# A graph attention and mixture-of-experts kernel: probabilities divided before their transposes instead of after the attention product

## The reference

```
n = layernorm(x)
q, k, v = n @ Wq.T, n @ Wk.T, n @ Wv.T + bv          # 12 heads of 32
a = softmax(q @ k.T * 384**-0.5 + adj)                # per head; a row that is all zero gives zeros
x = x + (a @ v) @ Wo.T + bo
```

```
u = layernorm(x)
y = u + sum over the 2 chosen experts e of gate_e * (act_e(u @ w1[e] + b1[e]) @ w2[e] + b2[e])
x = x + layernorm(y) * ln_g + ln_b
```

## Time and profile before

| what | value |
| --- | --- |
| median of three runs | 1617.83 us |
| profiled execution, its own time | 1619.34 us |
| its span, first to last instruction | 1617.5 us |
| mean granted TensorE clock | 0.998 of full speed |
| TensorE busy (matmul) | 1586.6 us, 98% |
| VectorE, ScalarE, GpSimd busy | 1194.9, 970.5, 687.1 us |
| chain that ended last: TensorE | 89% of the span |
| attention loop | to about 705 us; VectorE, ScalarE and GpSimd are each 70 to 90% busy in it |
| experts | from 705 us on; GpSimd is 10% busy |

### The profile page before, as it was taken

One profiled execution on the slowest core, in us unless ns is written; L12 is line 12 of the kernel. 1 busy time (PEld: TensorE's weight loads), 2 busy tenths in 40 slices (PEclk: granted clock), 3 DMA queues, 4 the chain that ended last, 5 costly groups with the idle time before them and its releaser, 6 DMA issues.

```text
span 1617.5 us, 44743 instructions
## 1 busy us (share of the span) xinstructions
PE 1586.6 (98%) x12720; PEld 1524.0 (94%) x12720; DVE 1194.9 (74%) x3754; ACT 970.5 (60%) x2880; POOL 687.1 (42%) x1105
## 2 busy tenths in 40 slices
PE   8999999999999999989999999999999999999998
PEld 7999999999999999879999999999999999999998
DVE  5787788878887778777766666676777767677776
ACT  6899999988999988863433333344344433344442
POOL 3777887778777877731111111111111111111112
PEclk9999999999999999999999999999999999999999
DMA  5433333344444433682211111111111111111211
GB/s 181 161 121 124 104 118 116 130 155 152 155 158 145 152 132 116 211 341 84 60 59 53 56 59 60 56 59 61 61 60 46 60 60 56 60 60 52 67 47 45
DMA packets 93512, 163.87 MB, mean 101 GB/s; under 512 B 10305, under 2 KB 73793, under 8 KB 92097
## 3 DMA queue, kind: packets, MB, share of 16 engines
q1 hardware_dynamic: 91664, 145.01, 27.2%
q10 hardware_dynamic: 1584, 15.73, 2.7%
HBM read 96.22 MB, written 64.49 MB: 99 GB/s over the span
## 4 chain that ended last, share of the span: by engine, by line
PE 89%; DVE 4%; ACT 2%; issue 2%; DMA 1%; DVEq 1%; POOL 0%; ACTq 0%; POOLq 0%; SPq 0%
PE bank L495 69%; PE bank L570 5%; PE bank L709 5%; PE bank L522 3%; PE bank L593 3%; PE bank L610 2%; PE bank L579 1%; PE bank L602 1%; DVE half_t L1458 1%; DVE inverse L1465 1%; DVE inverse L1461 1%; ACT inverse L1009 1%; ACT at_hi L1002 1%; ACT prob L781 1%; DVE hid L1339 0%
## 5 line engine op out<-in xcount | busy, mean ns | idle before, releaser
L495 PE MATMUL bank<-w_hi,ut_in 128*128 x1536 | 421.2, 341 | 0.4 <-issue 0.4
L495 PE MATMUL bank<-w_both,at_hi 128*128 x1524 | 390.0, 336 | 8.7 <-DVE at_lo L1430 8.0
L781 ACT ACTIVATE prob<-att,heads 128x128 f32<-128x128 f32 x768 | 297.5, 393 | 15.3 <-DVE heads L1182 12.3
L495 PEld LDWEIGHTS bank<-w_both,at_hi 128*128 128x128 f32 x1524 | 275.1, 188 | 14.3 <-issue 14.3
L495 PEld LDWEIGHTS bank<-w_hi,ut_in 128*128 128x128 f32 x1536 | 279.5, 188 | 1.4 <-issue 1.4
L495 PE MATMUL bank<-w_lo,ut_in 128*128 x768 | 256.9, 335 | 0.0
L495 PE MATMUL bank<-w_both,at_lo 128*128 x762 | 255.7, 336 | 0.0
L926 ACT ACTIVATE hid<-hid 128x384 f32<-128x384 f32 x192 | 95.1, 526 | 257.2 <-DVE hid L1339 256.5
L1002 ACT ACTIVATE at_hi<-bank,gate_col 128x384 fp32r<-128x384 f32 x254 | 133.4, 576 | 191.0 <-PE bank L709 189.1
L1158 POOL TENSOR_TENSOR xz<-xz,lnb_wide 128x384 f32<-128x384 f32 x64 | 67.6, 1057 | 405.6 <-DVE xz L1496 384.0
L1430 DVE SCALAR_TENSOR_TENSOR at_lo<-bank,gate_col,at_hi 128x384 fp32r<-128x384 f32 x254 | 144.8, 612 | 112.5 <-ACT at_hi L1002 112.5
(11 more groups left out here) (139 smaller groups left out, 3482.3 us busy)
## 6 DMA issues: line engine op xcount, KB each, us to landing
xu_scratch<-xu SPq DMA_DIRECT2D x64, 384.0 KB, 2.3
xz<-xu_scratch SPq DMA_DIRECT2D x64, 384.0 KB, 3.3
x_in<-in_x SPq DMA_DIRECT2D x32, 384.0 KB, 3.3
xu<-in_x SPq DMA_DIRECT2D x32, 384.0 KB, 4.3
ut_scratch<-ut_out SPq DMA_DIRECT2D x64, 192.0 KB, 1.9
ut_in<-ut_scratch SPq DMA_DIRECT2D x64, 192.0 KB, 2.3
out_dram<-xz SPq DMA_DIRECT2D x64, 192.0 KB, 1.9
w_lo<-in_L_ffn_w SPq DMA_DIRECT2D x4, 1152.0 KB, 6.1
```

Source lines behind the costliest of these rows:

```text
L495: last = nc.tensor.matmul(acc, lhs[c][a], rhs[c][b], start=start and n == 0, stop=stop and n == len(terms) - 1)
L781: nc.scalar.activation(prob[g][:, hh, :], att[g][:, head, :], ACT.Exp, bias=neg_max[g][:, head:head + 1], scale=-1.0, accum_out=row_sum[g] ...
```

## The change

The reciprocals are multiplied into the exponentials, before these are transposed. Removed are `spread_inverse`, `take_inverse`, `divide`, the spreading reduce in `invert_sums`, and the tiles `inv_t`, `inv_sum`, `ot`. New is a multiply of 128x512 (four heads) per group: group 0 on GpSimd, groups 1 and 2 on VectorE, in place in `prob`. `attend` writes bank 5, from which `round_o` (ScalarE) and `rest_of_o` (now VectorE) read directly. The sums, reciprocals and guards of zero rows are kept in the order in which the probabilities lie. TensorE's transposes of a group wait for its multiply. On GpSimd `root2` stands ahead of the multiply; on VectorE `rest_of_o`, the reciprocal and the multiply of group 1 stand ahead of `rest_of_x`. In the first graph ScalarE does `split_act_hi` of the first job before `activate` of the second. The lists of ScalarE and VectorE behind the loop are reordered. The diff, cut to its core:

```diff
             def project_qk(h):
-                reached(pe, ot_done, h - 1)
-                reached(pe, inv_taken, h - 1)
                 for oc in range(DC):
+                    if oc == 2:
+                        reached(pe, ot_lo_done, h - 1)
...
             def transpose_probs(n, c):
-                reached(pe, exp_done, HEADS * n + HPB * (c + 1))
+                if c == 0:
+                    reached(pe, scaled_pool, n + 1)
+                else:
+                    reached(pe, scaled_vec, 2 * n + c)
...
             def attend(n):
-                reached(pe, ot_done, n)
+                reached(pe, ot_lo_done, n)
-                        last = nc.tensor.matmul(bank[4][...], v_sb[...], pt[...], start=True, stop=True)
+                        last = nc.tensor.matmul(bank[5][...], v_sb[...], pt[...], start=True, stop=True)
...
             def round_o(n):
-                reached(act, ot_done, n + 1)
+                reached(act, o_mm, n + 1)
-                nc.scalar.activation(flat(ot_hi[g][:]), flat(ot[g][:]), ACT.Copy).then_inc(ot_hi_done, 1)
+                nc.scalar.activation(flat(ot_hi[g][:]), bank[5][:, 0:D], ACT.Copy).then_inc(ot_hi_done, 1)
...
-            exps(B - 1, (0, 1, 2, 3))
-            take_inverse(B - 2)
+            exps(B - 1, (0, 1, 2))
+            take_probs(B - 2, 0)
+            take_probs(B - 2, 1)
+            exps(B - 1, (3,))
             load_under_scores()
...
+                        if isinstance(b, int) and (b, k) == (0, 1):
+                            split_act_hi(0, 0, 0)
                         if not isinstance(b, int) or (b, k) != (0, 0):
                             activate(b, k, e)
...
+            def scale_probs(n):                      # GpSimd
+                reached(pool, inverse_ready, n + 1)
+                tile = prob[n % 2][:, 0:HPB, :]
+                nc.gpsimd.tensor_tensor(tile, tile, inverse_sum[:, 0:HPB].rearrange("p (h o) -> p h o", o=1).to_broadcast([P, HPB, N]),
+                                        ALU.mult).then_inc(scaled_pool, 1)
...
             for h in range(STEPS.start, B):          # GpSimd
-                if 0 <= h - 2 < B - 3:
-                    rest_of_o(h - 2)
                 if has(h - 1):
                     guard_sums(h - 1)
+                if has(h - 3) and h < B - 2:
+                    root2(h - 3)
+                if has(h - 1):
+                    scale_probs(h - 1)
                 if has(h - 2):
                     add_output_bias(h - 2)
-                if has(h - 3) and h < B - 2:
-                    root2(h - 3)
                 if has(h):
                     fold_scores(h)
...
             def invert_sums(n):                      # VectorE
                 reached(dve, guard_done, n + 1)
-                nc.vector.reciprocal(inverse_sum[:], guarded[:]).then_inc(inv12_done, 1)
-                dve.wait_ge(inv12_done, n + 1)
-                nc.vector.tensor_reduce(inv_sum[g][:], ...).then_inc(inv_done, 1)
+                reached(dve, scaled_pool, n)
+                reached(dve, scaled_vec, 2 * n)
+                nc.vector.reciprocal(inverse_sum[:], guarded[:]).then_inc(inverse_ready, 1)
+
+            def scale_probs(n, c):
+                dve.wait_ge(inverse_ready, n + 1)
+                tile = prob[n % 2][:, HPB * c:HPB * (c + 1), :]
+                nc.vector.tensor_tensor(tile, tile, inverse_sum[:, HPB * c:HPB * (c + 1)]...to_broadcast([P, HPB, N]),
+                                        ALU.mult).then_inc(scaled_vec, 1)
...
                 if has(h):                           # VectorE's loop
                     add_bias_and_max(h, (0, 1))
+                if 0 <= h - 2 < B - 3:
+                    rest_of_o(h - 2)
+                if has(h - 1):
+                    invert_sums(h - 1)
+                    scale_probs(h - 1, 1)
                 if has(h + 4):
                     rest_of_x(h + 4)
...
                 if has(h):
                     add_bias_and_max(h, (2, 3))
                 if has(h - 1):
-                    invert_sums(h - 1)
+                    scale_probs(h - 1, 2)
...
-                if has(h - 1):
-                    divide(h - 1)
                 if has(h + 2):
                     take_v(h + 2)
+                if h - 1 == B - 3:
+                    rest_of_o(h - 1)
...
             add_bias_and_max(B - 1, (0, 1, 2, 3))
             invert_sums(B - 2)
-            for c in range(PTC):
-                take_probs(B - 2, c)
+            scale_probs(B - 2, 1)
+            scale_probs(B - 2, 2)
             residual(B - 3)
-            divide(B - 2)
+            take_probs(B - 2)
             greatest_part(B - 1)
-            take_probs(B - 1)
+            rest_of_o(B - 2)
             invert_sums(B - 1)
-            rest_of_ut(0, 0, 0)
+            scale_probs(B - 1, 1)
+            scale_probs(B - 1, 2)
             sum_nodes(B - 4)
             residual(B - 2)
-            divide(B - 1)
+            take_probs(B - 1)
+            rest_of_ut(0, 0, 0)
+            rest_of_o(B - 1)
             rest_of_ut(1, 1, 0)
```

More of the change, by code:

```diff
@@ L128, in gnn_moe_kernel @@
         pt = [sb(f"pt{c}", [P, BANK], F32, s1) for c in range(PTC)]
-        inv_t = sb("inv_t", [P, DC, N], F32, s1)
-        inv_sum = [sb(f"inv_sum{g}", [P, HEADS, HEAD], F32, s1) for g in range(2)]
-        ot, ot_hi, ot_lo = [], [], []
+        spare = sb("spare", [P, 4 * D], F32, s1)
+        ot_hi, ot_lo = [], []
         def attended(g):
-            ot.append(sb(f"ot{g}", [P, DC, N], F32, s1))
             ot_hi.append(sb(f"ot_hi{g}", [P, DC, N], F32R, s1))
@@ L571, in transpose_probs @@
                 last.then_inc(pt_mm, 1)
[L573 to L580, removed]
             def attend(n):
@@ L592, in attend @@
                         hh, head = r * DC + c, QUAD * c + r
-                        last = nc.tensor.matmul(bank[4][HEAD * r:HEAD * (r + 1), c * N:(c + 1) * N], v_sb[p][g][:, head * HEAD:(head + 1) * HEAD],
+                        last = nc.tensor.matmul(bank[5][HEAD * r:HEAD * (r + 1), c * N:(c + 1) * N], v_sb[p][g][:, head * HEAD:(head + 1) * HEAD],
                                                 pt[hh // HPB][:, (hh % HPB) * N:(hh % HPB + 1) * N], start=True, stop=True)
@@ L806, in take_u @@
                 nc.scalar.activation(flat(ut_out[g][:]), bank[3][:, 0:D], ACT.Copy).then_inc(ut_taken, 1)
-            def take_inverse(n):
-                reached(act, in_mm, n + 1)
-                reached(act, ot_done, n)
-                nc.scalar.activation(flat(inv_t[:]), bank[5][:, 0:D], ACT.Copy).then_inc(inv_taken, 1)
             def normalise_x(n):
@@ L955, in _ @@
                     take_u(h - 3)
-                if has(h - 1):
-                    take_inverse(h - 1)
                 if has(h + 5):
@@ L981, in _ @@
             nc.scalar.preload_act_table(ACT.Gelu)
-            take_inverse(B - 1)
             round_ut(1, 1, 0)
@@ L1027, in expert_step @@
                         split_act_hi(b - 1, 1, m - 1)
-                    if k == 1 and graph(b, 0):
+                    if k == 1 and graph(b, 0) and not (isinstance(b, int) and b == 0):
                         split_act_hi(b, 0, m)
@@ L1057, in _ @@
             pool.wait_ge(const_ready, 1)
-            def rest_of_o(n):
-                g = n % 2
-                reached(pool, ot_hi_done, n + 1)
-                reached(pool, wo_mm, n - 1)
-                nc.gpsimd.tensor_tensor(flat(ot_lo[g][:]), flat(ot[g][:]), flat(ot_hi[g][:]).bitcast(F32), ALU.subtract).then_inc(ot_lo_done, 1)
             def root1(n):
@@ L1136, in _ @@
             guard_sums(B - 1)
+            scale_probs(B - 1)
             root2(B - 3)
@@ L1251, in take_v @@
                     dve.wait_ge(bv_loaded, 16)
+                if n == B - 9:
+                    dve.wait_ge(logit_mm, 1)
                 reached(dve, v_mm, n + 1)
```

45 lines of the change are left out of this document (19 added, 26 removed).

## The result

| | before | after |
| --- | --- | --- |
| median of six runs each, on the same chip | 1619.05 us (1617.38 to 1619.48) | 1626.20 us (1625.24 to 1629.91) |
| ratio, 95% interval | | 1.005 [1.004, 1.006] |
| profiled execution, its span | 1619.34, 1617.5 us | 1626.34, 1624.5 us |
| mean granted TensorE clock | 0.998 | 0.994 |
| TensorE, VectorE, ScalarE, GpSimd busy | 1586.6, 1194.9, 970.5, 687.1 us | 1584.0, 1254.8, 945.5, 745.2 us |

A forecast was written before the change was run, and what follows sets the result against it. TensorE was taken to bound the loop steps, the chain of the other engines the tail. Terms -3.5 -0.6 +1.2 +8.0 -0.3 +0.8 = +5.6 on 1619.34 gave 1624.9, or 1623 us as median; range 1606 to 1641.

The forecast's parts named there:

- Three transposes, -0.33 per step: Attention loop, TensorE: three transposes of 0.11 us each go from its list, -0.33 us per step.
- The stall of 0.27 at `project_o`: Each step: TensorE waits 0.27 us for `rest_of_x`, now behind three more VectorE instructions; bounds 0.13 or 0.54.
- Steps 2 to 59, -3.5: 58 loop steps with both edits at net -0.06 us each: -3.5 us, bounds -12 and +12.
- The multiplies and who is first: Each step: VectorE's multiply takes 0.69 us, starts 0.05 before GpSimd's and holds it; GpSimd's 1.28, some 1.8 with holding.
- Start, +1.2: Step 1: transposes must now wait for guard, reciprocal and multiplies; +1.2 us, bounds 0 and 2.
- Tail, +8.0: Scores of graph 62 to first FFN matmul: divisions now in line, 30.1 us for 22.1; +8.0, 5 to 10.
- First job, -0.3: Earlier rounding removes a 2.17 us wait, but the second job's chain is late next; -0.3 us, bounds -2.2 and +1.
- Clock, +0.8: A longer tail may put a half-clock stretch where TensorE bounds: 0 or +1.7 us, +0.8 taken.
- the one without a stall: Loop steps: no stall at `project_o`, -0.33 us stays in 60 steps, -19.8 us: 1608 us; chance 0.20.
- The tail that gets no longer: Tail stays as long as before and the sooner rounding pays: 1613 us; chance 0.08.
- The slow GpSimd multiply: Loop steps: GpSimd's multiply takes twice 1.28 us and the first transposes wait: 1649 us; chance 0.14.
- GpSimd first, 1691: Loop steps: GpSimd gets SBUF first, VectorE's multiply and `rest_of_x` end later, +68 us: 1691 us; chance 0.06.

The follow-up runs named there:

- three_back: Changed kernel with three transposes of the identity per step, read by nobody, where `spread_inverse` stood; 1649.13 us, 1.0183 of the kernel before.
- x_first: Changed kernel with `rest_of_x` ahead of the reciprocal and the first multiply on VectorE; 1614.04 us, 0.9968 of the kernel before.
- idle_filled: Changed kernel with 16, 20, 32 and 20 unread transposes of the identity where TensorE waits in the tail; 1625.23 us, 1.0037 of the kernel before.
- before_round: Kernel before with only the first job's rounding moved ahead of the second job's activations; 1619.37 us, 1.000 of the kernel before.
- late_round: Changed kernel with the first job's rounding back behind the second job's activations; 1629.09 us, 1.0056 of the kernel before.
- gp_ahead: Changed kernel with VectorE's order reciprocal, `rest_of_x`, multiply, and GpSimd's multiply ahead of `root2`; 1644.77 us, 1.0156 of the kernel before.
- all_filled: Changed kernel with `rest_of_x` early, tail lists of VectorE, GpSimd and TensorE reordered, and 12, 12 and 10 idle transposes; 1608.39 us, 0.9935 of the kernel before.

## Why the prediction was right

1623 us was forecast, in a range of 1606 to 1641; the median is 1626.20. For the profiled execution the sum gave 1624.9, and it took 1626.34. That it came this close is in part luck: two stretches that no edit touches were shorter, by 1.8 and 0.5 us, and took back most of what the clock cost beyond its term. By its own steps:

- **Three transposes, -0.33 per step**: right; three_back puts 0.35 on.
- **The stall of 0.27 at `project_o`**: right in size and place. x_first has a step of 10.367, the 10.70 of before less 0.33, and 0.27 under the changed kernel's 10.640. The shown step has `rest_of_x` ending 4.31 us into it (4.30 worked out), and of the 0.27 some 0.20 lie ahead of `project_o`'s first matmul and 0.07 behind it. The other new wait, at the third block, costs nothing, as forecast.
- **Steps 2 to 59, -3.5**: -2.1 measured. The median step is the predicted 10.64, the mean 10.66. The difference lies in the steps of 10.67 and in the five longer ones; all five are longer in x_first too, beside its 10.367, and what makes them so was not looked for. Steps 60 and 61: -0.8 for -0.6.
- **The multiplies and who is first**: right. VectorE 0.69 as interpolated, and first by 0.05. GpSimd's was over-priced (1.04 not held, for 1.28, and 1.54 held, for some 1.8) and was done 4.74 us into the step, for 4.98; it was not waited for in the steps.
- **Start, +1.2**: +1.16 over the first two steps.
- **Tail, +8.0**: the chain was right in its links: transposes of 62 at 14.90 (15.05), of 63 at 23.73 (24.05), and with the clock kept up 30.22 to the first FFN matmul (30.1). The kernel as changed took 32.89. Attention 62, which stands beside the chain, came at 18.4 in idle_filled for 17.7.
- **First job, -0.3**: -0.1 to -0.3 by before_round and late_round, with the mish chain late next. The sign that went with it did not come: from the first FFN matmul to the second job's transposes 20.2 us was forecast (20.55 before), and it took 20.91, with half clock on the first layers; in idle_filled it took 19.56.
- **Clock, +0.8**: the term that was mis-sized. The stretch at half clock was 13.7 us and reached over the transposes and `project_o` that bound; idle_filled puts the price at 2.7 in the tail and 4.0 to the second job's transposes. I had taken a stretch of the length in the earlier trace rows as the longest that could come.
- The expert part after the second job's transposes is 1.8 us shorter after than before. No edit touches it, and it scattered between 876.4 and 878.3 in the runs' traces: not explained. The other 0.5 us lies ahead of the scores of graph 0.

Of the rivals, the one without a stall did not come, though one move away from it lies x_first. The tail that gets no longer did not come either (32.89 for 22.09). The slow GpSimd multiply did not come: 1.04 not held, 1.54 held. GpSimd first, 1691, did not come. gp_ahead shows its mechanism at work (1.34 and 1.43 for 0.69, the step from 10.37 to 10.88), by VectorE's whole list and not by `rest_of_x`, which stood ahead there. The case as the prediction had it, `rest_of_x` behind a held multiply, was not tried.

## What to carry to other kernels

Work taken from the bound engine pays in full only if what it then meets is also sooner: here 0.33 us per step was won and 0.27 lost, because an instruction of 0.55 us that TensorE waits for stood in VectorE's queue behind a reciprocal and a multiply. Putting it ahead of them was worth 15.9 us of steps in the trace and 12.2 in the median. A division that costs nothing beside a full TensorE becomes a link of the chain where the loop runs out; draw that chain link by link, and order each engine's last steps for it alone (32.9 to 27.4 us here, part of it by 6.8 us at half clock in place of 14). When an instruction is held by another engine, price all that stands behind it in its queue and close the loop to the next step.

## What the runs showed of the hardware that was not expected

- A GpSimd 512-wide multiply with a broadcast operand takes 1.04 us when not held, as much as a 384-wide add (1.01) and less than the 1.28 on the line between 384 and 768.
- The half granted clock (1.2 GHz) held on for 13.7 us in the changed kernel's tail, after waits of TensorE of 2.09, 1.25 and 2.73 us, and through 9.44 us of its work. In idle_filled, with those waits filled, 2.4 GHz was granted throughout the tail and to the second job's transposes. In all_filled, with fewer fillers, it was not: how much is enough was not found. Nor is the place fixed: late_round, with the same lists, had its first stretch 3.8 us after the scores of 62 and not 15.4. What it costs depends on who bounds there. In the changed kernel's trace it cost nothing up to the transposes of 63 and 2.7 us behind them; in late_round the early stretch made the scores of 63 0.74 late (9.74 for 9.00).
- Holding works on one-column instructions too: 0.77 for 0.27 (L1068) while VectorE multiplied.
- A held multiply does not wait for its whole length: GpSimd's ended 0.90 us after VectorE's in the step shown, and takes 1.04 when not held.
